# An attention kernel on one core: x loaded first, its first piece cut in two, GpSimd's order changed, reciprocals stored in another order

## What is computed

```python
q = einsum('oc,bcn->bon', Wq, xf) + bq      # 32 channels
k = einsum('oc,bcn->bon', Wk, xf) + bk      # 32 channels
v = einsum('oc,bcn->bon', Wv, xf) + bv      # 256 channels
scores = einsum('bqi,bqj->bij', q, k)       # 1024 x 1024 for each image
attn = softmax(scores, axis=-1)
out = einsum('bcj,bij->bci', v, attn) + x
```

## Time and profile before

| what | value |
|---|---|
| device time, three runs | 165.82 us median (165.29 to 167.39) |
| the profiled execution | 165.86 us, of which the profile's span is 164.1 us |
| TensorE matmuls busy | 157.8 us (96%) |
| VectorE, ScalarE, GpSimd busy | 134.5 us (82%), 109.4 us (67%), 56.6 us (34%) |
| granted TensorE clock, every one of 40 slices | full (the digit 9 in each) |

### The profile page before, as it was taken

One profiled execution on the slowest core, in us unless ns is written; L12 is line 12 of the kernel. 1 busy time (PEld: TensorE's weight loads), 2 busy tenths in 40 slices (PEclk: granted clock), 3 DMA queues, 4 the chain that ended last, 5 costly groups with the idle time before them and its releaser, 6 DMA issues.

```text
span 164.1 us, 2469 instructions
## 1 busy us (share of the span) xinstructions
PE 157.8 (96%) x797; PEld 131.9 (80%) x797; DVE 134.5 (82%) x214; ACT 109.4 (67%) x200; POOL 56.6 (34%) x66
## 2 busy tenths in 40 slices
PE   7799999999999999999999999999999999999993
PEld 5478778797688898788788898789888898888882
DVE  3599999886988989996999989895988679856851
ACT  3658998869799656746999665645896655756400
POOL 6079973344143303733343300241433300024600
PEclk9999999999999999999999999999999999999999
DMA  4586670452011130165310330053220330003003
GB/s 143 196 300 169 232 232 28 96 135 78 4 48 39 58 128 0 38 145 192 128 48 1 100 128 2 16 147 82 83 97 1 96 128 0 0 1 132 0 0 128
DMA packets 7636, 14.67 MB, mean 89 GB/s; under 512 B 1488, under 2 KB 1928, under 8 KB 7624
## 3 DMA queue, kind: packets, MB, share of 16 engines
q1 hardware_dynamic: 6872, 13.59, 25.7%
q0 software_dynamic: 608, 0.80, 2.3%
q10 hardware_dynamic: 144, 0.13, 0.2%
HBM read 4.79 MB, written 4.20 MB: 55 GB/s over the span
## 4 chain that ended last, share of the span: by engine, by line
PE 83%; POOL 7%; DMA 2%; ACT 2%; DVE 2%; issue 1%; SPq 0%; POOLq 0%; DVEq 0%; ACTq 0%
PE acc L970 30%; PE acc L976 16%; PE slot L823 10%; PE st L957 8%; PE slot L883 7%; PE slot L970 5%; POOL x_lo L409 3%; DMA x_sb<-x 2%; PE slot L976 2%; POOL x_hi L407 2%; PE slot L835 2%; PE slot L840 2%; DVE scaled L733 1%; ACT k_a L530 1%; POOL w_lo L401 1%
## 5 line engine op out<-in xcount | busy, mean ns | idle before, releaser
L401 POOL TENSOR_TENSOR w_lo<-w_full,w_hi 128x512 fp32r<-128x512 f32 x21 | 28.1, 1337 | 53.8 <-PE acc L976 34.1
L970 PE MATMUL acc<-w_hi,v_hi 128*128 128x512 f32 x112 | 44.7, 399 | 0.3 <-DVE scaled L733 0.2
L970 PE MATMUL acc<-w_hi,v_lo 128*128 128x512 f32 x112 | 44.2, 394 | 0.0
L518 ACT ACTIVATE w_full<-st 128x512 f32<-128x512 f32 x62 | 36.7, 592 | 7.2 <-PE st L957 7.1
L480 ACT ACTIVATE dump<-slot,negmax 128x1024 f32<-128x1024 f32 x29 | 32.4, 1119 | 10.4 <-DVE negmax L641 9.9
L641 DVE TENSOR_REDUCE negmax<-slot 128x1 f32<-128x1024 f32 x29 | 35.3, 1218 | 3.2 <-PE slot L883 2.8
L976 PE MATMUL acc<-w_lo,v_hi 128*128 128x512 f32 x112 | 36.5, 397 | 0.3 <-POOL w_lo L401 0.3
L707 DVE TENSOR_TENSOR w_lo<-w_full,w_hi 128x512 fp32r<-128x512 f32 x43 | 31.7, 740 | 3.3
L970 PEld LDWEIGHTS acc<-w_hi,v_hi 128*128 128x128 f32 x112 | 21.1, 189 | 6.7 <-issue 0.8
L976 PEld LDWEIGHTS acc<-w_lo,v_hi 128*128 128x128 f32 x112 | 21.0, 188 | 5.5 <-POOL w_lo L401 0.7
L970 PEld LDWEIGHTS acc<-w_hi,v_lo 128*128 128x128 f32 x112 | 21.2, 189 | 4.6
(11 more groups left out here) (103 smaller groups left out, 217.5 us busy)
## 6 DMA issues: line engine op xcount, KB each, us to landing
out<-x_sb SPq DMA_DIRECT2D x7, 512.0 KB, 2.8
x_sb<-x SPq DMA_DIRECT2D x3, 1024.0 KB, 6.1
k_b<-k_a SPq DMA_DIRECT2D x8, 192.0 KB, 2.6
q_b<-q_a SPq DMA_DIRECT2D x8, 192.0 KB, 2.7
x_sb<-x SPq DMA_DIRECT2D x2, 512.0 KB, 4.3
k_a<-qk_parts SPq DMA_DIRECT2D x12, 64.0 KB, 2.2
q_a<-qk_parts SPq DMA_DIRECT2D x12, 64.0 KB, 2.2
k_a<-qk_parts POOLq DMA_DIRECT2D x6, 64.0 KB, 2.1
```

The costliest lines, as they stand in the source:

```text
L401: nc.gpsimd.tensor_tensor(w_lo[:, r, :], w_full[:, r, :], w_hi[:, r, :].bitcast(fp32), ALU.subtract).then_inc(w_split_pool, 1)
L518: nc.scalar.activation(w_full[:, r, :], st_home(n), ACT.Exp).then_inc(exp_done, 1)
L970: nc.tensor.matmul(dst, v[:, b % 2, j, c * P:(c + 1) * P], w_hi[:, n % RING, part], start=(j == 0 and v is v_hi), stop=False)
```

## The change

Six edits:

1. `small` is issued from ScalarE's queue, ahead of its table load; x's first half is SP's first DMA.
2. ScalarE cuts the first piece of x in two quarters (five cuts for four). The first projection multiplies the high parts of that piece quarter by quarter; everything else still takes it whole, so the counts waited for grow by one.
3. 22 idle matmuls are issued ahead for 17.
4. GpSimd cuts x1's last quarter, then makes the low weights of its tiles among the first two (n = 1), then splits x1's last quarter.
5. `inv_row` is written in the order of the pixels, element by element.
6. So `inv_all` is read with unit stride in `finish(0, 0, c)`.

```diff
+        FIRST_PIECES = ((0, quarter(0)), (0, quarter(1)), piece(1), piece(2), piece(3))
...
         @block.sync
         def _(sp):
-            sp.dma_start(small_sb[:, :], small).then_inc(small_in, DMA)
             for c in range(CT):
...
             sp.wait_ge(inv_ready, 1)
-            sp.dma_start(inv_row.rearrange("(p t) -> p t", p=P), inv[:, :]).then_inc(inv_put, DMA)
+            with nc.allow_non_contiguous_dma("512 numbers, long ahead of their use"):
+                sp.dma_start(inv_row.rearrange("(t p) -> p t", p=P), inv[:, :]).then_inc(inv_put, DMA)
...
-            def prepare_x1(i):
+            def cut_x1(i):
                 if i == 0:
                     pool.wait_ge(x1_in, DMA)
                 nc.gpsimd.tensor_copy(x_hi[:, 1, :, quarter(i)], x_sb[:, 1, :, quarter(i)]).then_inc(x1_cut, 1)
+
+            def split_x1(i):
                 pool.wait_ge(x1_cut, i + 1)
...
-            prepare_x1(3)
+            cut_x1(3)
+            pool.wait_ge(x1_cut, 4)
+
+            for n in range(AHEAD):
+                split_w(n)
+            pool.wait_ge(w_split_pool, 1)
+            split_x1(3)
             pool.wait_ge(x1_split, 4)
-            for n in range(TILES):
+            for n in range(AHEAD, TILES):
...
         def _(act):
+            act.dma_start(small_sb[:, :], small).then_inc(small_in, DMA)
             act.preload_act_table_set("natural_log_exp_and_others")
-            for i in range(4):
-                c, part = piece(i)
+            for i in range(5):
+
+                c, part = FIRST_PIECES[i]
                 act.wait_ge(x0_in[c], DMA)
...
-                dve.wait_ge(x0_cut, i + 1)
+                dve.wait_ge(x0_cut, i + 2)
...
-                    nc.vector.tensor_tensor(scaled[:, c, :].rearrange("p (t q) -> p t q", t=TH),
-                                            acc[:, c, :].rearrange("p (t q) -> p t q", t=TH),
-                                            inv_all[:, :].rearrange("p (q t) -> p t q", t=TH),
+                    nc.vector.tensor_tensor(scaled[:, c, :], acc[:, c, :], inv_all[:, :],
                                             ALU.mult).then_inc(acc_read, 1)
...
                 if i == 0:
                     pe.wait_ge(wqk_cut, 1)
-                pe.wait_ge(x0_cut, i + 1)
-                nc.tensor.matmul(dst, wqk_hi[:, c, :], x_hi[:, 0, c, part], start=(c == 0), stop=False)
-                if i == 0:
+
+                    for a in range(2):
+                        pe.wait_ge(x0_cut, a + 1)
+                        nc.tensor.matmul(dst[:, quarter(a)], wqk_hi[:, c, :], x_hi[:, 0, c, quarter(a)],
+                                         start=(a == 0), stop=False)
                     pe.wait_ge(wqk_split, 1)
+                else:
+                    pe.wait_ge(x0_cut, i + 2)
+                    nc.tensor.matmul(dst, wqk_hi[:, c, :], x_hi[:, 0, c, part], start=(c == 0), stop=False)
                 nc.tensor.matmul(dst, wqk_lo[:, c, :], x_hi[:, 0, c, part], start=False, stop=False)
...
-            keep_busy(17, QUARTER)
+            keep_busy(22, QUARTER)
```

More of the change, by code:

```diff
@@ L429, in _ @@
             pool.wait_ge(q2_lo_put, 1)
-            prepare_x1(0)
+            cut_x1(0)
+            split_x1(0)
             pool.wait_ge(x1_split, 1)
-            prepare_x1(1)
+            cut_x1(1)
+            split_x1(1)
             pool.wait_ge(x1_split, 2)
             pool.wait_ge(shift_ready, 1)
-            prepare_x1(2)
+            cut_x1(2)
+            split_x1(2)
             pool.wait_ge(x1_split, 3)
-            prepare_x1(3)
+            cut_x1(3)
[4 more added lines that the diff above has]
+            split_x1(3)
             pool.wait_ge(x1_split, 4)
-            for n in range(TILES):
+            for n in range(AHEAD, TILES):
                 b, more = n // PER, n // PER + 1 < BATCH
```

## The result

The changed kernel takes 168.74 us (median of six, 168.14 to 169.79), the kernel before 165.91 in the same rounds: a ratio of 1.016, with a 95% interval of 1.010 to 1.022. So it is slower, by 2.8 us by the medians, where 1.5 us less were forecast. Three executions far off all others (223.12 and 259.72 us in two of the experiments, 396.77 us of the kernel before) count in no median here. The profiled execution took 169.63 us, 3.8 us more than that of before.

A forecast was written before the change was run, and what follows sets the result against it. TensorE was taken to bound the kernel, with time to win only at three gaps: 0.30 (start) + 0.44 (tile 1) + 0.75 (scalings) = 1.49 us off 165.86, giving 164.4 us; own range 164.1 to 164.7, full range 163.7 to 165.3.

The forecast's parts named there:

- The scalings: VectorE's two scalings at acc's refill, 41 us: 0.69 us each with contiguous reciprocals instead of 1.07, winning 0.75 us.
- the sum: Gains at start, tile 1 and scalings, 0.30 + 0.44 + 0.75 = 1.49 us, taken from 165.86 to 164.4 us.
- part 4: Reciprocals in contiguous order: faster scalings win 0.75 us at acc's refill; the store in 512 4-byte pieces costs 0.
- Four times that is 0.3 us: landing in about 1.65 us: Reciprocals' store on SP's queue: 0.08 us of packet time times four; landing 1.65 us for 1.4, about 2 us of cover.
- 1.4 x 4 = 5.6 us: Store's landing if every part grew with the piece count: a stall of 0.9 us and a time of 165.3 us.
- the scattered write lands late: Rival, chance 0.04: SP waits for the store, delaying image 1's stack copies; landing up to 4.7 us is free.
- part 3: GpSimd makes w_lo of tile 1 before x1's last split: TensorE's stall at 23.8 us goes, winning 0.44 us.
- what is late next: After tile 1's stall: tile 6's scores need ScalarE's row sum, 0.15 us remains; x_lo's last quarter is wanted after 31 us.
- parts 1 and 2: Start: x issued first lands 0.35 us earlier, quarters cost 0.05, longer idle cover 0; TensorE wins 0.30 us.
- the longer cover: 22 idle matmuls for 17 before the first projection, ending at 5.7 or 5.2 us: cost 0 to 0.1 us, taken as 0.
- 2 us of cover: Small, used by VectorE at 2.58 us but by TensorE only after 5 us, was said to have 2 us to spare.
- Quarters worth nothing: Halving ScalarE's first cut of x: cost on the path to x_lo between 0 and 0.22 us, taken as 0.05.

The follow-up runs named there:

- the last version: Kernel before with edits 1 to 3, x1's last split waiting for VectorE's w_lo of tile 4, 16-byte store, ScalarE reordering the reciprocals: 164.36 us, ratio 0.990.
- the start edits alone: Kernel before with edits 1 to 3 only (x first, small on ScalarE's queue, quarters, 22 idle matmuls): 165.62 us, ratio 0.9945.
- the probe: Kernel before with reciprocal stores of several forms, then VectorE operations alone and beside GpSimd's, behind its end; 512 side-by-side 4-byte pieces took 8.5 us, its time not compared.

## Why the prediction was wrong

**The gaps read from the rows were there.** The start: 0.30 forecast at the first matmul on x_lo, 0.33 in the trace, though not by the forecast's terms and not in the time (below). Tile 1's stall: 0.44 forecast, 0.49 measured where nothing takes its place. The scalings: 0.75 forecast, 0.77 measured. The version that has them without their side effects takes 164.36 us; the sum had said 164.4. That these two agree so closely is partly luck: the sum started from 165.86 us and counted 0.30 for the start, while the last version lies 1.26 us below 165.62, the start edits alone. What failed are two costs put at nothing, and one step about the start.

**The store (part 4).** "Four times that is 0.3 us: landing in about 1.65 us" scaled the packets' time, and the packets are indeed quick: all 528 were through between 25.7 and 26.4 us by the DMA view, in under 1 us. The landing isn't the packets; for 6.7 us afterwards the engines show next to no work while SP waits. The bound of the prediction, 1.4 x 4 = 5.6 us, was worked out too, and its rival ("the scattered write lands late") named the right queue and the right mechanism, with a chance of 0.04; free it would have been up to 4.7 us. An operation whose form no row of before shows can't be priced from the part of a near row that one can explain; the bound had to be the whole landing, and more. Even so the rival's price was short: it counted SP's wait alone. The measured landing of 7.9 us would have made a stall of 3.2 us by its sum at k_a's copies (1.9, since the store went out at 25.12 us and not at 26.5). There TensorE did stand in two other kernels with this store, for 3.1 and 3.7 us. In the changed kernel it stood 2.46 us before that, for the shift rows that GpSimd had issued in time, since DMAs of GpSimd's queue landed late after the store as well (5.4 us for 2.0). And it left out what a stall can do to TensorE's clock: in this trace another 1.5 us at the lower level, by the executions' times (median 169.71 for 168.53) 1.2 us in two of six. By the medians, 2.4 us net remain of it.

The Trainium skill, page "DMA: Bandwidth & Descriptors", section "Specifications", says that below 512 bytes the engine reads, modifies and writes. That both forms are below it, as the prediction said, is so; the probe shows that the rule doesn't order them: 16-byte pieces land in 1.4 us, 4-byte ones side by side in 8.5, spaced ones in 1.8 to 2.9.

**GpSimd's order (part 3).** The step "what is late next" looked at who waits for GpSimd and for ScalarE's sum, not at what GpSimd's moved work runs beside. Moved by 1.9 us to 23.02 us, the x1 subtraction lies beside VectorE's cast and subtraction of tile 2; these grow by 0.89 and 0.93 us, TensorE's wait at tile 2 takes the place of the one at tile 1, and 0.8 us are lost where 0.44 were to be won. The trace of before had a sign: the cast of x1's last quarter took 1.10 us, beside VectorE's subtraction of tile 0, and 0.61 elsewhere. The Trainium skill states it, page "SBUF — State Buffer", section "Who interferes with whom": VectorE and GpSimd share a port pair, a VectorE cast can be shut out for a whole GpSimd instruction, an instruction with two SBUF inputs contends with one of GpSimd's that reads SBUF, and a subtraction with one SBUF input doesn't. The changed kernel's trace agrees (the cast ends 0.28 us after GpSimd's subtraction), and so does the probe (1.75 for 0.68 us with two SBUF inputs, 0.68 unchanged with one and PSUM).

**The start (parts 1 and 2).** The place and its 0.3 us were right for the profiled execution, and the sum was made against that one execution. But x's first cast began anywhere from 4.39 to 5.35 us in five traces with x issued second, and from 4.43 to 4.55 in eight with x first: the profiled one was at the late side (5.11). Against the lower group of the kernel before (165.2 to 166.4, its medians 165.4 to 165.6) the start edits win nothing, 165.6. What they do is take away the upper group, 34 of 76 executions, 1.4 to 1.7 us above the lower. The prediction saw that 17 idle matmuls ran at the pace of 1.2 GHz and put the longer cover at 0 to 0.1 us of cost; it did not ask whether the kernel before may meet its first projection at that pace, since the profiled execution hadn't. Nor did it foresee that small would be 2.1 us later: bounded at 2 us of cover, it used that cover up, and VectorE's x_lo now starts when the weights are done, not when x is cut. So two terms were off and made up for each other in the trace, which is luck: x's cast came 0.63 us earlier (0.35 forecast), and about 0.3 of it went to the late weights, a cost put at nothing (without quarters as well: cast at 4.53, matmul at 6.25 us). Whether small placed elsewhere would win that back no run tried. Quarters worth nothing: as forecast.

**The sum over all**, by medians: start edits 165.62; GpSimd's order +0.76; store and scalings +2.36; 168.74. Not settled: why the DMAs of other queues land late after the store (inv_all, which reads what it wrote, stands between them; no run left that out), and what in DRAM makes neighbouring 4-byte writes slow; only the time of each was measured.

## What to carry to other kernels

A DMA is not priced by its bytes or packets: if a change gives it a form that no row shows, take the whole landing as unknown, list what stands behind it on its queue, and probe the form by itself. Work moved on GpSimd is priced twice: by who waits for it, and by which VectorE instructions that read SBUF it now runs beside. And a stall of TensorE of 2 to 3 us can cost more than its length, since the lower clock may follow, while a layout can often be put right where an idle engine does it in SBUF.

## What the runs showed of the hardware

- Stores to DRAM of 4-byte pieces side by side land in 7.0 us (128 pieces) and 7.9 to 8.5 us (512; 9.4 with a 1 MB load issued behind it), spaced by 64 bytes in 2.9 (measured right behind a slow one), by 512 bytes in 1.8, to SBUF in 2.1; of 16-byte pieces in 1.4. A 1 MB load issued just behind such a store took 14.3 us instead of 4.7.
- VectorE's multiplication with one input read at a stride of 16 bytes in SBUF takes 1.07 us, with unit stride 0.68. ScalarE's copy of the same strided 512 columns takes 1.13 us.
- 66 KB on ScalarE's queue beside 1 MB on SP's lands in 3.9 us, alone ahead of it in 1.8.
- TensorE's pace at the start varies between executions, with the printed granted clock 1.00 in all: the first projection ran at 0.43 us for 512 columns until 9.1 to 9.6 us in three traces, where TensorE had stood for 0.72 to 1.26 us before it while still at the low pace; until 6.6 to 7.0 us in three traces without such a gap; and at 0.23 from 6.9 us at the latest in seven.
- After 2.46 us without a matmul, the granted clock was 0.50 for some 3 us in the profiled execution; four of the kernel's six executions have a mean granted clock of 1.00.
